# TensorE's program written out for all 256 steps, its waits carried by its products

## The reference, cut to what matters

```python
def _gn(v, G=32, eps=1e-5): ...            # groups of 2 channels: (v - mean) / sqrt(var + eps)

# layer 0: depthwise 3x3, then three 64x64 channel matrices
dw = conv3x3_depthwise(_gn(x), depthwise_weights)
att = softmax(attention_weights) @ dw
pw = pointwise_weights @ att
x = x + softmax(global_attention_weight) @ pw

# layer 1: 3x3 convolution of signs with signs, scaled by one mean |w| per output channel
x = x + conv3x3(sign(_gn(x)), sign(clip(w, -1, 1)) * mean(abs(clip(w, -1, 1))))
```

## Time and profile before

| | |
|---|---|
| median of 3 runs | 1886.92 us (1886.14 to 1887.1) |
| profiled execution, its own time | 1885.17 us |
| its span, first to last instruction | 1883.3 us |
| mean granted TensorE clock | 0.999 of full |
| TensorE products | 33132, busy 1768.4 us (94% of the span) |
| TensorE weight loads | 33132, busy 1506.3 us (80%) |
| VectorE, ScalarE, GpSimd | busy 85%, 71%, 30% |
| first layer-0 product | starts at 99.3 us |

### The profile page before, as it was taken

How to read it: one execution, slowest core, us unless ns; L and a number is a source line. 1 busy time by engine, 2 the same in 40 slices (tenths; PEclk the granted TensorE clock), 3 DMA queues, 4 the chain that set the end, 5 groups by cost and what they waited for, 6 DMA issues and landing times.

```text
span 1883.3 us, 76437 instructions
## 1 busy us (share of the span) xinstructions
PE 1768.4 (94%) x33132; PEld 1506.3 (80%) x33132; DVE 1600.8 (85%) x2634; ACT 1336.3 (71%) x1463; POOL 574.0 (30%) x341
## 2 busy tenths in 40 slices
PE   0089999999999999999999999999999999999997
PEld 0079777899988877889988888789998788888996
DVE  5668889888898889988899888988899888877776
ACT  2067776777777777777777777777777777677774
POOL 0033332333333333323333333333333333233331
PEclk9999999999999999999999999999999999999999
DMA  9925665565565665555655666556655666432334
GB/s 204 220 72 147 167 153 140 166 152 154 146 156 158 157 154 145 150 156 152 154 144 159 157 156 156 137 158 156 156 145 147 164 152 154 104 89 69 78 78 102
DMA packets 279264, 271.39 MB, mean 144 GB/s; under 512 B 16576, under 2 KB 278848, under 8 KB 279104
## 3 DMA queue, kind: packets, MB, share of 16 engines
q1 hardware_dynamic: 279104, 269.23, 56.2%
HBM read 134.95 MB, written 134.22 MB: 143 GB/s over the span
## 4 chain that ended last, share of the span: by engine, by line
PE 85%; DVE 7%; SPq 4%; issue 2%; ACT 1%; DMA 1%; DVEq 0%; ACTq 0%
PE psA L499 73%; PE psB L499 12%; SPq L260 3%; DVE bnt L720 1%; ACT xh L376 1%; DVE ring L920 1%; DVE ring L886 1%; DMA ring<-in_x 1%; DVE psL L916 1%; DVE pk L897 1%; DVE aggr L827 1%; DVE xc L878 1%; ACT xn L372 0%; SPq L267 0%; DVE sums L731 0%
## 5 line engine op out<-in xcount | busy, mean ns | idle before, releaser
L499 PE MATMUL psA<-xh,W 64*64 64x512 f16 x17912 | 1549.2, 373 | 16.5 <-ACT xh L376 11.9
L499 PEld LDWEIGHTS psA<-xh,W 64*64 64x64 f16 x17912 | 1067.0, 106 | 149.4 <-issue 71.5
L499 PE MATMUL psA<-xl,W 64*64 64x512 f16 x9216 | 984.9, 376 | 0.0
L312 POOL TENSOR_TENSOR xl<-xc,xn 128x1024 f16<-128x1024 f32 (+1 forms) x320 | 571.1, 1794 | 1228.7 <-ACT xn L372 1228.7
L499 PEld LDWEIGHTS psA<-xl,W 64*64 64x64 f16 x9216 | 578.3, 107 | 51.6 <-issue 0.6
L499 PE MATMUL psB<-pk,W 64*64 64x512 f16 (+1 forms) x4944 | 604.0, 362 | 2.3 <-DVE pk L897 1.9
L376 ACT ACTIVATE xh<-xc 64x1024 f16<-64x1024 f32 (+2 forms) x624 | 577.0, 942 | 9.3
L372 ACT ACTIVATE xn<-xc 128x1024 f16<-128x1024 f32 (+2 forms) x264 | 272.1, 1034 | 276.5 <-PE psA L499 191.2
L886 DVE SCALAR_TENSOR_TENSOR ring<-psA,columns,ring 128x1024 f32<-128x1024 f32 x256 | 328.2, 1282 | 141.2 <-PE psA L499 140.7
L720 DVE BATCH_NORM_STATS2 bnt<-ring 128x6 f32<-128x512 f32 x512 | 326.8, 680 | 49.2 <-DMA ring<-in_x 48.9
L499 PEld LDWEIGHTS psB<-pk,W 64*64 64x64 f16 x4944 | 298.1, 106 | 64.5 <-issue 51.0
(11 more groups left out here) (90 smaller groups left out, 133.5 us busy)
## 6 DMA issues: line engine op xcount, KB each, us to landing
out_y<-ring SPq DMA_DIRECT2D x512, 256.0 KB, 3.3
ring<-in_x SPq DMA_DIRECT2D x448, 256.0 KB, 4.0
ring<-in_x SPq DMA_DIRECT2D x32, 512.0 KB, 13.9
pk<-in_w1T SPq DMA_DIRECT2D x2, 144.0 KB, 7.8
ring<-in_w1n SPq DMA_DIRECT2D x2, 144.0 KB, 7.6
grp<-in_same_group SPq DMA_DIRECT2D x1, 64.0 KB, 6.1
ring<-in_dw SPq DMA_DIRECT2D x2, 2.2 KB, 5.6
ring<-in_att SPq DMA_DIRECT2D x1, 16.0 KB, 2.1
```

What stands on the lines that cost most here:

```text
L312: ins = nc.gpsimd.tensor_tensor(xl[:, slot:slot + rows, 1:W + 1], xc[:, j:j + rows], xn[:, k:k + rows, 1:W + 1], ALU.subtract)
L499: mm = pe.matmul(bank[out0:out0 + C, c0:c1], weights[src0:src0 + C, :], src[src0:src0 + C, slot:slot + rows, width[0]:width[0] + width[1]] ...
```

## The change

The loop is replaced by steps written out (100 steps of text become 256). The function `turn` emits the semaphore increment only if the count of the wait is not a plain integer. With every step written out all counts are integers, so no increment is emitted, and a wait is carried by the next instruction, the weight load of the product that follows. Where two waits stand together, an instruction has room for one of them: in the kernel before, the pair of waits ahead of L464 stands as one semaphore instruction at L463 and one wait on the weight load of L464. The products, their order and the numbers waited for are the same.

```diff
+            def turn(count):
+                if not isinstance(count, int):
+                    pe.sem_inc(bank_turns, 1)
+
             def bank_free(sem, count):
                 pe.wait_ge(sem, count)
-                pe.sem_inc(bank_turns, 1)
+                turn(count)
...
                 if j == 12:
                     pe.wait_ge(xl_rdy, n + 1)
-                    pe.sem_inc(bank_turns, 1)
+                    turn(n)
...
                 if j == 6:
                     pe.wait_ge(xl_rdy, n + 1)
-                    pe.sem_inc(bank_turns, 1)
+                    turn(n)
...
                     if not (isinstance(n, int) and n < 2):
                         pe.wait_ge(suma_rdy, n - 1)
-                    pe.sem_inc(bank_turns, 1)
+                    turn(n)
...
                 if not (isinstance(n, int) and n < 2):
                     pe.wait_ge(a_post, n - 1)
-                pe.sem_inc(bank_turns, 1)
+                turn(n)
...
             def image(img, first):
                 for i in range(4 * first):
                     step(img, i, (lambda: mean_average(img)) if i == 0 else None)
-                with pe.Fori(first, NC // 4 - 1) as v:
-                    for q in range(4):
-                        step_one(img, Chunk(v, q), img, Chunk(v, q - LAG))
+                for i in range(4 * first, NC - 4):
+                    step(img, i)
                 for i in range(NC - 4, NC):
                     step(img, i, (lambda: gather_stats(img + 1)) if i == GROUP_STEP and img + 1 < NB else None)
```

## The result

The changed kernel takes 1878.47 us (median of 9 runs, 1875.98 to 1882.04), the kernel before 1886.92 us in the 9 runs beside them. The ratio is 0.9958, 95% interval 0.9949 to 0.9967: faster by 0.42%, where 1904 us was forecast. The span of the profiled execution, from its first to its last instruction, is 1874.9 us against 1883.3.

A forecast was written before the change was run, and what follows sets the result against it. TensorE's products were taken to bound the kernel, hiding branches and semaphore instructions. From 1885.2 us, less 7 of old stalls, plus 27 for late fetches: 1905 profiled, about 1907 as median, shaded to 1904; range 1880 to 1915.

The forecast's parts named there:

- the second of "the change, part by part": TensorE's weight queue, every step: seven semaphore instructions become two; 65 us leave the queue, 0 us leave the products.
- The fetches' term: TensorE's program, 261 blocks in place of 104: late blocks cost 27 us (12 to 42); the earlier 7 us go out.
- The unseen places: About 20 block-border places in the step that no row shows, between bad and good ones; priced at 0.75 us each.
- The rival that came true is the first: Fetches are hidden once loops and semaphore instructions are gone, so the stalls vanish: 1880 us, faster by 4 to 8, chance 0.28.
- the even stretches: Written-out steps of images 2, 4 and 6: block borders fall half a step away, 13 blocks fetched, no issue stall.

## Why the prediction was wrong

**What bounds the kernel, and what the stalls were: right.** Products at 6.82 us per step before and after, the loops' branches free (the kernel with loops ties with the one without), the 4.8 us on issue being late blocks of TensorE's program, 261 blocks forecast and 260 fetched. Where blocks come late, the stalls depend on the place of the border in the step, and grow as it slips.

**The step that failed** is the second of "the change, part by part": "5 x 51 ns x 256 = 65 us leave the weight queue and 0 us leave the products". I priced a semaphore instruction by its own 51 ns, found them covered, and wrote "the same waits now block the weight load in the same place, so what queues behind them is the same". It isn't: weight loads idle on issue fell from 73.4 and 51.0 us to 9.8 and under 1, and blocks began at 291 instructions at the latest, where it had been 419. Put back into the written-out kernel, the same instructions bring 46.3 us of idle time and blocks at up to 448. What the change takes away was the cause of the lateness that I charged to the blocks.

**The fetches' term** (27 us, less the 7 of before) took a price per block, measured with all seven such instructions in the step, into a kernel that has none with wait and increment together: there the term measured 0. For the kernel to which it applies, the one written out with the increments kept, it had the sign and was too small: 65 us over the changed kernel where the sum had 27. The unseen places beyond those of the earlier trace rows were bad as well, and the bad part of the step was some 100 instructions wide (48 to 145), where I had set 50. That these 65 us equal the 65 us that were to leave the weight queue is chance: the same seven increments of 51 ns, ahead of the waits, cost nothing.

**The rival that came true** is the first, given 0.28: 1880 us, measured 1878.47, and of its three possible causes (semaphore instructions, branches, entering a loop) the semaphore instructions. I held against it that "the semaphore instructions are as many in the even stretches, which don't stall". That was no evidence: the even stretches had borders at good places, by the prediction's own reading. It takes both, these instructions and a border at a bad place, and the argument used the one against the other.

**The Trainium skill.** Its page "Runtime: NRT & Kernel Launch", section "Instruction fetch mechanics", says that crossing a 16 KiB border is mostly hidden, and that a taken branch to code outside the current two pages forces a fetch before execution can go on. On the first the changed kernel agrees (260 blocks, no product idle on issue), and with it the forecast's 27 us would have been 0; in the kernel written out with its increments one block in five isn't hidden (57 stalls at 265 blocks, 46.3 us). On the second no run here agrees: a loop's body is over four blocks long, no block is fetched again for it, and with 47 branches left in the time is the same, 1877.62.

**What stays open.** Shown is that waits held by semaphore instructions which also increment, with no wait on the weight load behind, make the next block's fetch late, most of all at the bank waits together with the low part's; and that with the increment apart or gone, and a second wait on the weight load, no more than some 3 us are lost. Which of these two differences it is, and by what mechanism a fetch gets late, stays open; so does why lateness keeps to one part of the step.

## What to carry to other kernels

Look for the cause of a stall before you multiply it: a price read off rows holds only while all that stands beside it stays, and here the part taken away was what made the price. Let the weight loads carry the products' waits. If a wait needs an instruction of its own, keep the increment out of it, and let the weight load behind carry a wait too, as in the runs that lost little here. Look at code that runs once, for a loop's body of this length was fetched only in its first pass. To tell two halves of a change apart, run each alone: together they gave 0.4%, one alone the same, and the other alone a loss of 3.0%.

## What the runs showed of the hardware

- TensorE's instructions come in packets of 256. In the changed kernel packet k started when 256 k + 161 to 256 k + 291 instructions had begun, and it is needed at 256 k + 449. Loops of four steps (some 1,060 instructions, over four packets) were not fetched again.
- Seven semaphore instructions of 51 ns per step, each a wait with an increment and all covered by products, cost 65 us in 256 steps written out, since blocks of the program then come late (up to 448 in place of 291). Their own duration says nothing on that.
- Beside 6.82 us of products, twelve semaphore instructions per step that don't combine wait and increment are hidden. With fourteen, seven of which combine them, the step takes 6.96 us; whether by number or kind is not shown.
- Weight loads that wait 107.5 us in all for issue cost hardly any product time (1878.76 us, products idle on issue 0.6 us), as long as blocks come in time.
